# Query and key projections with a 512-column moving operand, their parts added on VectorE

## The reference, cut to what matters

```python
q = (x @ Wq + bq).reshape(b, n, H, HD)
k = (x @ Wk + bk).reshape(b, n, H, HD)
v = (x @ Wv + bv).reshape(b, n, H, HD)
scores = jnp.einsum('bihd,bjhd->bhij', q, k) / jnp.sqrt(jnp.float32(HD))
scores = scores + mask[None, None, :, :]
weights = jax.nn.softmax(scores, axis=-1)
out = jnp.einsum('bhij,bjhd->bihd', weights, v)
```

## Time and profile before

| what | value |
|---|---|
| median of three runs | 2746.28 us (2746.20 to 2747.28) |
| the profiled execution's own time | 2746.01 us |
| its span, first to last instruction | 2744.2 us |
| PE busy | 2677.5 us, 98% |
| PE weight loads busy | 2404.0 us, 88% |
| DVE busy | 1925.9 us, 70% |
| ACT busy | 1474.4 us, 54% |
| POOL (GpSimd) busy | 1483.6 us, 54% |
| mean granted TensorE clock | 0.993 |

### The profile page before, as it was taken

One profiled execution on the slowest core, in us unless ns is written; L12 is line 12 of the kernel. 1 busy time (PEld: TensorE's weight loads), 2 busy tenths in 40 slices (PEclk: granted clock), 3 DMA queues, 4 the chain that ended last, 5 costly groups with the idle time before them and its releaser, 6 DMA issues.

```text
span 2744.2 us, 60531 instructions
## 1 busy us (share of the span) xinstructions
PE 2677.5 (98%) x19593; PEld 2404.0 (88%) x19593; DVE 1925.9 (70%) x6165; ACT 1474.4 (54%) x4360; POOL 1483.6 (54%) x1806
## 2 busy tenths in 40 slices
PE   4899999999999999999999999999999999999996
PEld 3799899889889889989988988988998998898896
DVE  7777776776777776777767767767777777767753
ACT  3355555555555555555555555555555555555554
POOL 5655555555555555555555555555556555555541
PEclk9999999999999999999999999999999999999998
DMA  4000000000000000000000000000000000000000
GB/s 124 15 22 28 28 24 27 27 24 27 24 27 27 19 29 30 20 27 31 19 27 31 20 27 31 20 27 31 20 27 27 24 27 27 24 27 27 13 16 24
DMA packets 41607, 75.19 MB, mean 27 GB/s; under 512 B 5584, under 2 KB 5712, under 8 KB 41424
## 3 DMA queue, kind: packets, MB, share of 16 engines
q1 hardware_dynamic: 41424, 73.49, 8.3%
HBM read 39.92 MB, written 33.55 MB: 27 GB/s over the span
## 4 chain that ended last, share of the span: by engine, by line
PE 96%; DVE 1%; issue 1%; ACT 1%; DMA 0%; POOL 0%; ACTq 0%; SPq 0%; POOLq 0%; DVEq 0%
PE rot L796 24%; PE rot L798 23%; PE rot L797 23%; PE score L917 5%; PE rot L904 5%; PE rot L853 4%; PE rot L889 4%; PE rot L939 2%; PE rot L952 2%; PE rot L873 2%; PE rot L877 2%; PE s_bank L861 0%; PE att_bank L945 0%; DMA probs<-in_L_gnn_W 0%; DVE x L644 0%
## 5 line engine op out<-in xcount | busy, mean ns | idle before, releaser
L338 POOL TENSOR_TENSOR ve<-mv,eps_col 128x1 f32<-128x1 f32 (+1 forms) x448 | 88.1, 197 | 695.5 <-ACT e L503 352.8
L796 PE MATMUL rot<-w_hi,y_hi 128*128 128x512 f32 x1024 | 425.2, 415 | 5.6 <-DVE y_lo L634 4.7
L360 POOL TENSOR_TENSOR x2b<-x,bias 128x512 f32<-128x512 f32 x128 | 203.5, 1590 | 416.4 <-DVE x L644 416.4
L798 PE MATMUL rot<-w_hi,y_lo 128*128 128x512 f32 x1024 | 404.8, 395 | 0.0
L797 PE MATMUL rot<-w_lo,y_hi 128*128 128x512 f32 x1024 | 404.2, 395 | 0.0
L549 ACT ACTIVATE probs<-score,sc_nmax 128x128 f32<-128x128 f32 x1024 | 357.0, 371 | 11.4 <-DVE sc_nmax L757 11.4
L796 PE MATMUL rot<-xt_hi,wk_hi 128*128 128x256 f32 x1024 | 299.8, 293 | 0.0
L634 DVE TENSOR_TENSOR y_lo<-rot,y_hi 128x512 fp32r<-128x512 f32 x128 | 88.5, 691 | 296.4 <-ACT y_hi L467 296.4
L798 PE MATMUL rot<-xt_hi,wk_lo 128*128 128x256 f32 x1024 | 290.2, 283 | 0.0
L798 PE MATMUL rot<-xt_hi,wq_lo 128*128 128x256 f32 x1024 | 289.8, 283 | 0.0
L797 PE MATMUL rot<-xt_lo,wq_hi 128*128 128x256 f32 x1024 | 289.7, 283 | 0.0
(11 more groups left out here) (117 smaller groups left out, 7758.5 us busy)
## 6 DMA issues: line engine op xcount, KB each, us to landing
x_in<-in_x SPq DMA_DIRECT2D x128, 256.0 KB, 2.6
out_x<-x SPq DMA_DIRECT2D x128, 256.0 KB, 2.2
probs<-in_L_gnn_W SPq DMA_DIRECT2D x1, 1024.0 KB, 8.0
v_sb<-in_L_gnn_weight SPq DMA_DIRECT2D x1, 1024.0 KB, 7.1
probs<-in_L_gnn_Wv SPq DMA_DIRECT2D x1, 1024.0 KB, 5.4
v_sb<-in_L_gnn_Wq SPq DMA_DIRECT2D x1, 1024.0 KB, 5.3
probs<-in_L_gnn_Wk SPq DMA_DIRECT2D x1, 1024.0 KB, 5.4
x<-in_L_gnn_a SPq DMA_DIRECT2D x1, 512.0 KB, 5.7
```

The costliest lines, as they stand in the source:

```text
L360: pool.tensor_tensor(x2b[:, :], x2[:, slot.buf(L_GCN, 2), :], bias2[:, :], ALU.add)\
L796: pe.matmul(outp, lh, rh, start=first, stop=False)
L798: return pe.matmul(outp, ll, rh, start=False, stop=last)
```

## The change

The two halves of the transposed x3 are put into one tensor so that for one feature block the upper and the lower half of the two graphs can be read as one moving operand of 2 x 256 = 512 columns. The products w_hi x (xt_hi, xt_lo) then come from one matmul of 512 columns: its first 256 columns hold w_hi x xt_hi, its last 256 columns w_hi x xt_lo. The third product, w_lo x xt_hi, is a matmul of 256 columns onto the first 256 columns of the same bank. Each of the two output blocks of a projection so fills a bank of its own: queries use `rot[0]` and `score_bank[0]`, keys `rot[2]` and `score_bank[1]`.

The two parts of each output block are added when they are moved to SBUF: ACT moves the second half of the bank with the bias as before (and counts `q_part_done` or `k_part_done`), then DVE adds the first half of the bank onto it in SBUF (`join_parts`, two instructions a projection) and counts `q_done` or `k_done`. On DVE the query join stands directly ahead of `y1_lo` (634), the key join directly behind the first layer's aggregate (603) and ahead of the reciprocal 685. PE's wait for `score_exp` of the slot before moves from the scores to the middle of each projection.

```diff
-        xt_hi = sb("xt_hi", [P, KC, BUFS, P], F32R)
-        xt_lo = sb("xt_lo", [P, KC, BUFS, P], F32R)
+        xt = sb("xt", [P, KC, 2, BUFS, P], F32R)
+        xt_hi, xt_lo = xt[:, :, 0, :, :], xt[:, :, 1, :, :]
...
-        def q_bank(c):
-            return rot[0][:, c * GROUP * P:(c + 1) * GROUP * P]
-
-        def k_bank(c):
-            return rot[2][:, c * GROUP * P:(c + 1) * GROUP * P]
+        PAIR = GROUP * P
+        q_bank = (rot[0], score_bank[0])
+        k_bank = (rot[2], score_bank[1])
...
-                        ins = biased(q_sb[:, c, :], q_bank(c), qb_col[:, chunk:chunk + 1])
-                    ins.then_inc(q_done, 1)
+                        ins = biased(q_sb[:, c, :], q_bank[c][:, PAIR:2 * PAIR], qb_col[:, chunk:chunk + 1])
+                    ins.then_inc(q_part_done, 1)
...
+            def join_parts(dst, banks):
+
+                for c, bank in enumerate(banks):
+                    ins = dve.tensor_tensor(dst[:, c, :], bank[:, 0:PAIR], dst[:, c, :], ALU.add)
+                return ins
...
+                if slot.on(L_QK):
+
+                    slot.wait(dve, q_part_done, L_QK)
+                    join_parts(q_sb, q_bank).then_inc(q_done, 1)
                 if slot.on(L_GAT):
                     slot.wait(dve, y1_hi_done, L_GAT)
...
                     aggregate("0", slot.buf(L_EDGE, 2))
+                if slot.on(L_QK):
+
+                    slot.wait(dve, k_part_done, L_QK)
+                    join_parts(k_sb, k_bank).then_inc(k_done, 1)
                 if slot.on(L_ATT):
...
-            def projection(bank, w, slot):
+            def projection(banks, w, slot):
 
+                w_hi, w_lo = weights[w]
                 first = slot.buf(L_QK, BUFS) // GROUP * GROUP
-                for c in range(CHUNKS):
+                for c, bank in enumerate(banks):
                     chunk = slot.part(L_QK) * CHUNKS + c
+                    cols = slice(chunk * P, (chunk + 1) * P)
+                    if c == 1:
+                        slot.wait(pe, score_exp, L_QK, 1)
                     for k in range(KC):
-                        ins = three(bank[:, c * GROUP * P:(c + 1) * GROUP * P],
-                                    [a[:, k, chunk * P:(chunk + 1) * P] for a in weights[w]],
-                                    [b[:, k, first:first + GROUP, :].rearrange("p g n -> p (g n)") for b in (xt_hi, xt_lo)],
-                                    k == 0, k == KC - 1)
+                        pe.matmul(bank[:, 0:2 * PAIR], w_hi[:, k, cols],
+                                  xt[:, k, :, first:first + GROUP, :].rearrange("p t g n -> p t (g n)"),
+                                  start=k == 0, stop=False)
+                        ins = pe.matmul(bank[:, 0:PAIR], w_lo[:, k, cols],
+                                        xt_hi[:, k, first:first + GROUP, :].rearrange("p g n -> p (g n)"),
+                                        start=False, stop=k == KC - 1)
                 return ins
...
-                    slot.wait(pe, score_exp, L_QK, 1)
                     for c in range(CHUNKS):
```

More of the change, by code:

```diff
@@ L219, in graph_layers_kernel @@
         wa_done = sem("wa_done")
+        q_part_done, k_part_done = sem("q_part_done"), sem("k_part_done")
         setup_mm, setup_copied = sem("setup_mm"), sem("setup_copied")
@@ L480, in emit @@
                         chunk = slot.part(L_QK) * CHUNKS + c
-                        ins = biased(k_sb[:, c, :], k_bank(c), kb_col[:, chunk:chunk + 1])
-                    ins.then_inc(k_done, 1)
+                        ins = biased(k_sb[:, c, :], k_bank[c][:, PAIR:2 * PAIR], kb_col[:, chunk:chunk + 1])
+                    ins.then_inc(k_part_done, 1)
                 if slot.on(L_ATT):
@@ L840, in emit @@
                     slot.wait_last(pe, (edge_max_done, L_EDGE, 1), (pt1_done, L_PV, 1))
-                    projection(rot[0], "wq", slot).then_inc(q_mm, 1)
+                    projection(q_bank, "wq", slot).then_inc(q_mm, 1)
                 if slot.on(L_GAT):
@@ L865, in emit @@
                     slot.wait_last(pe, (xt_lo_done, L_TR, 1), (y2_lo_done, L_GCN, 1), (k_done, L_QK, 1))
-                    projection(rot[2], "wk", slot).then_inc(k_mm, 1)
+                    projection(k_bank, "wk", slot).then_inc(k_mm, 1)
                 if slot.on(L_PV):
```

## The result

| | us, median (range) | runs | against the kernel before |
|---|---|---|---|
| before | 2746.64 (2746.20 to 2747.28) | 4 | |
| changed | 2728.84 (2728.18 to 2730.51) | 4 | ratio 0.9936, interval 0.9919 to 0.9953 |

What follows compares the result with a forecast made beforehand. Matmul issue on PE was taken as the bound. From 2746.01 us, 25.6 for fewer projection matmuls and 4 for a removed wait gave 2716.4, 2716.7 as a median; range 2707 to 2729.

Steps and rivals of the forecast that it cites:

- the 18.8 that the sum had as its lower bound: Projections on PE: least gain, 18.8 us, if long matmuls cost 230.0 ns as in the drain; the removed wait giving 0.
- the 2 us kept for the fill and the drain: Fill and drain: allowance of 2 us in the range's slow end, in case a join shows in PE's chain there.
- What bounds the kernel: Outside fill and drain, only PE's matmul issue sets the time; PE busy for 100.00 of 100 us in a middle window.
- The price of a matmul as the distance of starts: PE's matmuls: each costs about 12.5 ns independent of columns, plus 107.1 ns for each 256 columns.
- Rival (a): Projections: a long matmul costs about what two short ones do, 239 ns, so they save nothing; 2742 to 2746 us, 4%.
- I take 25.6, because both of its terms are of full streams in the same part of the slot.: Query and key projections: each group of three matmuls falls from 358.8 to 346.3 ns, saving 25.6 us over 128 slots.
- The wait removed ahead of the scores, 4 us: Ahead of the scores on PE: removing one of three waits saves 0.03 us a slot, 4 us, bounds 0 and 11.5.
- Added waits, ACT: Waits in the middle of the projections cost PE 0; ACT's copies keep size, order and start, so no cost.
- rival (b): Middle of the projections: added waits break PE's lead, taking back 23 of the 29.6 us; about 2740 us, 4%.
- The joins: DVE's four new additions a slot: about 416 ns each, 0.76 us a pair, costing PE nothing; least slack 0.42 us.
- Rival (c): Key join comes too late and PE stands at line 889 every slot: 74 us lost, 2790 us, 4%.
- Its small stalls: Late key join stalls PE at line 889 only a little, leaving part of the gain: 2728 to 2740 us, 3%.

Runs made afterwards that it cites:

- q_only: The changed kernel with the key projection and its copy as before, without the key join, so only the queries are changed: 2737.52 us, ratio 0.9970.
- grouped: The changed kernel with each output block's four 512-column matmuls first, then its four 256-column ones, in place of alternation: 2721.05 us, ratio 0.9909.
- wait_back: The changed kernel with a third, already satisfied wait for score_exp put back ahead of the scores: 2728.97 us, ratio 0.9939.
- k_only_wait: k_only with one unneeded, satisfied wait for score_exp added in the middle of the query projection: 2744.19 us, one run.
- no_key_wait: The changed kernel without the score_exp wait in the middle of the key projection: 2728.09 us, one run.
- transpose_ahead: The changed kernel with one unneeded 128x128 fp32 transpose right ahead of the query projection: 2740.31 us, ratio 0.9980.
- k_only: The changed kernel with the query projection, its copy and q_done as before, so only the keys are changed: 2742.65 us, ratio 0.9989.

## Why the prediction was right in kind and 12 us off in size

The time, 2728.84 us, lies 0.2 inside the forecast's 2707 to 2729, and that is luck: the gain of 17.8 us is below the 18.8 that the sum had as its lower bound, and only the 2 us kept for the fill and the drain, which cost nothing, cover it. The steps one by one:

- **What bounds the kernel.** Right. The slot's 140 ns times 128 are 17.9 us, and the median moved by 17.8.
- **The price of a matmul as the distance of starts, 12.5 ns beside its columns.** Right. The keys' group takes about the forecast's 346.3 ns (347 from 230 + 117), and with widths grouped all 25.6 us come: 2746.74 - 2721.05 = 25.7. Rival (a) falls with it. The Trainium skill, "TensorE: Matmul & The Clock Gate", section Back-to-back issue gap, gives 2.5 ns beside the columns for an isolated gap. This stream disagrees: by that figure the projections would give 5 us, an estimate.
- **"I take 25.6, because both of its terms are of full streams in the same part of the slot."** This is the step that failed: the term measured (62 + 100) x 128 = 20.7 us. A pure stream of 512 columns has 226.7 ns and a pure one of 256 has 119.6, but a mixed stream isn't their sum. In the queries the distances repeat over three pairs, 232 118, 241 120, 236 113 ns: 353 ns a pair. With the first pairs, that is 2811 ns instead of 2873 - 100 = 2773: 38 x 128 = 4.9 us. My upper bound for a group's cost, 349.6 ns, was itself taken from a stream of one width and lies below this.
- **What stands behind the projections unchanged.** The prediction gave it no term. The edge product and dense products together cost 15 + 11 - 3 = 23 ns a slot, 2.9 us. q_only shows that what was changed with the keys brings it, and grouped, with the key join in place, that the order of widths alone does: between the keys and the edge product stand 60 other matmuls, so the effect reaches far down the stream.
- **The wait removed ahead of the scores, 4 us.** Wrong: 0, by wait_back. The stop there doesn't depend on whether two or three waits stand at it. That it belongs to the change of tile shape is likely, but no run here shows it.
- **Added waits, ACT.** Right at 0: the waits by k_only_wait and no_key_wait, and rival (b) falls; ACT by its busy time and by PE's window without a gap.
- **The joins.** Right at 0, and right in their sizes: 0.39 to 0.42 us each, a pair in 0.72 (0.76 forecast), slack 0.58 us in the slot shown and 0.52 in the mean of its kind (0.42 forecast), 1.16 in the other kind (0.95). Rival (c) falls. Its small stalls would have given this time as well (2728 to 2740); that PE waited for a key join once in the whole run is what rules them out. Its price was overstated: for a pair 1.26 us later it had 74 us, while four additions, 1.32 us, cost 18.4 in the median and 13.4 by the slots (two cost 3.7 and 5.1). The Trainium skill says in "SBUF — State Buffer", section Who interferes with whom, that a DVE instruction with at most one SBUF input, outside the two-port modes, does not contend with GpSimd, and that one with two SBUF inputs contends with a GpSimd instruction that reads SBUF. The trace agrees: the joins, with one operand in PSUM, take 390 to 417 ns where they overlap a POOL instruction and 390 to 425 where they don't, and line 659, with two in SBUF, has the waits shown above.

Missing are 4.0 + 4.9 + 2.9 = 11.8 us, and 29.6 - 17.8 = 11.8. (The fit is closer than its terms are known: the slot's distances make it 90 ns, 11.5 us.)

Open: what inside PE makes the rhythm. It isn't the waits tried, nor joins, weights or banks. Other engines are unlikely: the queries' pattern is the same in the drain of the changed kernel, from 2666.00 to 2668.80 us, where DVE is busy for 0.31, ACT for 0.60 and POOL for 0.04 of 2.80 us, as from 1415.00 to 1417.80, where they are for 1.69, 0.60 and 1.28. That loads and matmuls take turns in a fixed order with a period of several matmuls is a guess that fits; no run here shows it.

## What to carry to other kernels

Where PE is the bound, two narrow matmuls that share a stationary operand are worth merging: each one that goes saves about 12.5 ns here, and the addition was free on a DVE that had 0.5 us of slack where PE wants the sum. Then keep matmuls of one width together, since alternating widths gave back 38 of 100 ns of the gain in the queries' own stream and 23 ns more behind the keys; try two or three orders and time the whole kernel, because a stream's rhythm depends on the one before. Read such effects as mean distances by position in a period, not as durations, and expect a slack read from a trace to be soft where the chain ahead of it can shrink.

## What the runs showed of the hardware that was not expected

- An alternating stream of 512 and 256 columns has at least three stable patterns, one of 353 ns a pair and two of about 347, picked by the matmuls that ran before. One transpose switched it (transpose_ahead), and so did other queries ahead of the keys (k_only).
- When a stream of split operands begins behind plain fp32 matmuls, its distances are 313, 224, 231, 236, 228, 232, 231 ns before they settle at 227 (dense 1 of the changed kernel), 1695 ns where seven settled ones take 1587; before, the same product starts 314, 231, 236, 228, 232, 231. The stream before also had 128 columns a matmul; whether the type or the width does it was not separated.
- The load side's stop ahead of the scores, 0.17 us a slot, is the same with two waits and with three.
- The same DVE instruction, line 659's, had a mean of 871, 756 and 386 ns in three kernels that differ by nothing but two or four more additions elsewhere on DVE. It meets the same POOL addition in every slot, and either takes 0.28 us or ends 0.15 us behind POOL's end.
